# Masked attention: a cast moves from DVE to ScalarE, a subtraction moves behind the slot's second maximum, and four stages fetch their constants ahead of a norm

## The reference

```
x = x + tanh(g_xattn[l]) * attention_l(layernorm(x), context)
x = x + tanh(g_ffn[l])   * feed_forward_l(layernorm(x))
```

## Time and profile before

| | |
|---|---|
| Device time, median of 3 runs | 6104.12 us (6094.38 to 6107.08) |
| The profiled execution | 6067.9 us, span 6066.1 us |
| PE, DVE, ACT, POOL busy | 87%, 74%, 53%, 30% of the span |
| Granted TensorE clock, mean | 0.94 |
| Masked attention's loop | about 137 us to 1480 us of the span |

### The profile page before, as it was taken

How to read it: one execution, slowest core, us unless ns; L and a number is a source line. 1 busy time by engine, 2 the same in 40 slices (tenths; PEclk the granted TensorE clock), 3 DMA queues, 4 the chain that set the end, 5 groups by cost and what they waited for, 6 DMA issues and landing times. The chain is left out here.

```text
span 6066.1 us, 133138 instructions
## 1 busy us (share of the span) xinstructions
PE 5274.8 (87%) x51447; PEld 3802.1 (63%) x51447; DVE 4463.3 (74%) x9176; ACT 3196.1 (53%) x6024; POOL 1847.1 (30%) x1447
## 2 busy tenths in 40 slices
PE   3998998988679999989849999999999759999997
PEld 1777777777268878877824444444444437878885
DVE  7888888886367777763457777777777557777776
ACT  1666666666246666652224444444444226666663
POOL 5776767672122222212101111111111022222220
PEclk6999999999789999989969999999999879999998
DMA  5555555553267777742010000000000049889981
GB/s 128 131 125 128 125 129 127 126 128 76 49 129 139 135 142 142 140 88 105 25 31 20 16 15 15 15 15 15 15 15 10 8 101 158 158 163 162 162 157 25
DMA packets 369567, 545.00 MB, mean 90 GB/s; under 512 B 116084, under 2 KB 248310, under 8 KB 368806
## 3 DMA queue, kind: packets, MB, share of 16 engines
q1 hardware_dynamic: 366982, 533.81, 43.3%
q0 software_dynamic: 2048, 3.67, 0.2%
HBM read 413.45 MB, written 123.90 MB: 89 GB/s over the span
## 5 line engine op out<-in xcount | busy, mean ns | idle before, releaser
L696 DVE CUSTOM_DVE_ANT_0 attn_logits<-attn_scores,attn_shift 112x750 f32<-112x750 f32 x1024 | 945.6, 933 | 433.2 <-PE attn_scores L501 432.9
L614 ACT ACTIVATE attn_probs_t<-attn_pt 125x448 f32<-125x448 f32 x1536 | 831.0, 542 | 581.1 <-PE attn_pt L516 560.8
L516 PEld LDWEIGHTS attn_pt<-ident,attn_logits 112*125 112x125 f32 x6144 | 852.3, 189 | 178.6 <-issue 92.3
L516 PE MATMUL attn_pt<-ident,attn_logits 112*125 112x112 f32 x6144 | 921.1, 273 | 25.6 <-ACT attn_logits L605 24.5
L2329 PE MATMUL attn2k_pk<-attn_wk,attn2k_cn_t 128*125 128x512 f32 x1536 | 737.7, 602 | 39.6 <-ACT attn2k_cn_t L2400 36.8
L2340 PE MATMUL attn2k_pg<-attn2k_kn,attn2k_cn 125*128 125x512 f32 x1536 | 725.0, 594 | 4.5 <-ACT attn2k_gram L2408 2.3
L2495 DVE TENSOR_REDUCE attn2k_ss<-attn2k_sq 125x16 f32<-125x1024 f32 x384 | 467.0, 1216 | 255.2 <-ACT attn2k_sq L2437 255.1
L413 POOL CAST attn_k_parts<-xn_t 128x500 bf16<-128x500 f32 x192 | 206.5, 1075 | 1425.3 <-DVE xn_t L668 1425.3
L2437 ACT ACTIVATE attn2k_sq<-attn2k_pk 125x1024 f32<-125x1024 f32 x384 | 391.9, 1020 | 326.4 <-PE attn2k_pk L2329 326.2
L1228 ACT ACTIVATE attn_probs_t<-attn_pt 125x448 f32<-125x448 f32 x768 | 414.6, 540 | 281.2 <-PE attn_pt L1115 279.7
L2329 PEld LDWEIGHTS attn2k_pk<-attn_wk,attn2k_cn_t 128*125 128x125 f32 x1536 | 274.0, 187 | 399.2 <-issue 296.9
(11 more groups left out here) (371 smaller groups left out, 10444.4 us busy)
## 6 DMA issues: line engine op xcount, KB each, us to landing
attn_k_packed<-k_scratch SPq DMA_DIRECT2D x372, 375.0 KB, 6.3
attn_k_packed<-k_scratch SPq DMA_DIRECT2D x408, 187.5 KB, 4.4
k_scratch<-attn_k_parts SPq DMA_DIRECT2D x64, 1125.0 KB, 7.2
attn_ctx_t<-in_ctx_t SPq DMA_DIRECT2D x64, 750.0 KB, 7.3
k_scratch<-attn_k_parts SPq DMA_DIRECT2D x96, 375.0 KB, 3.7
attn_ctx_t<-in_ctx_t SPq DMA_DIRECT2D x96, 250.0 KB, 4.1
attn2k_ctx<-in_ctx SPq DMA_DIRECT2D x32, 750.0 KB
attn_mask_in<-in_mask SPq DMA_DIRECT2D x192, 109.4 KB
```

The source lines that it names most:

```text
L516: last = pe.transpose(pt[(3 * at + t) % 2][0:KC, (c % 4) * PAIR:(c % 4 + 1) * PAIR], logits[:, at % 3, c * KC:(c + 1) * KC], g.ident[0:PAI ...
L614: act.activation(probs_t[0:KC, p // 4, 4 * t:4 * t + 4, (p % 4) * PAIR:(p % 4 + 1) * PAIR], pt[(3 * at + t) % 2][0:KC, 0:QUAD].rearrange(" ...
L696: dve.tensor_tensor_reduce(out=logits[:, at % 3, cols].rearrange("p (b k) -> p b k", b=2), in0=scores[h][0:PAIR, :, 0:QTR], in1=shift[:, n ...
```

## The change

In the masked attention, `take_keys` on DVE keeps only the copy of the finite elements for the sequences from n = 2 on. The cast is issued by ACT (`high`), after the second `exp` and `lower` of slots 2 to 4 (and after `keep` in slot 2). The subtraction stays on DVE (`rest`), but stands behind the slot's second `shifted` instead of in front of it. For the first two sequences, which are prepared ahead of the loop, all three stay on DVE in the old order.

```
 ACT, slot p, after exp(.., 1) and lower(.., 1):
+    if t == 1 and 2 <= p < 5 and n + 2 < B:
+        high(n + 2, p - 2)
+def high(n, i):                      # on ACT
+    at = 3 * n + i
+    act.wait_ge(k_ready, at + 1)
+    if at > 1:
+        act.wait_ge(k_stored[at % 2], 16 * (at // 2))
+    act.activation(k_parts[:, at % 2, 0, :], clean_k[at % 2], ACT.Copy).then_inc(high_ready, 1)
 DVE, slot p:
     shifted(n, p, 0)
     take(n + 2, p - 2) ... finite ... mark
     shifted(n, p, 1)
+    if 2 <= p < 5 and n + 2 < B:
+        rest(n + 2, p - 2)
```

Four stages now take a function `ahead`, which is their norm. They allocate their SBUF tiles, issue their loads in Blocks of their own, in which nothing waits for the data, call `ahead()`, and allocate PSUM tiles and run as before:

```
+def fetch(nc, pairs, landed):
+    with nc.Block() as block:
+        @block.sync
+        def _(sp):
+            for dst, src in pairs:
+                sp.dma_start(dst, src).then_inc(landed, 16)
 ffn0:      fetch(6 loads); ahead()
 mixture:   fetch(router, order, bias); fetch(experts [, their bias]); ahead()
 attention2 (and ln1 gain and shift by a fetch before it, no longer waited for):
+  fetch(wv_t, wo, wq, wk, bo); fetch(gain, shift); fetch(first context tile); ahead()
 attn2q, first instructions of the engines:
+  DVE:  context_stats(0) in four steps, context_scales(0)
+  ACT:  context_root(0), context_normed(0) for all 12 chunks, then the copies of w_vo
+  POOL: context_affine(0), i.e. gain and shift
 attn2k: the same work for n = 0 is left out there; loads start with n = 1
```

More of the change, by code:

```diff
@@ L130, in _, with norm @@
                 act.wait_ge(tanhs, 1)
[L133 removed]
+def norm(nc, g, name, gate=None, out=None, twice=None, only_y=None, rows=None, twice_in=None):
     r = scope(nc, name)
@@ L1389, in take @@
                         take_keys(n, i)
+                        if n < 2:
+                            high(n, i)
+                            rest(n, i)
                     else:
@@ L1585, in ffn0 @@
                  (gate[:], a["gate0"].partition_broadcast(RANK))]
+        fetch(nc, loads, loaded)
+        ahead()
+        pw = [r.ps("pw0", [128, 512]), r.ps("pw1", [128, 512])]
+        pl = [r.ps("pl0", [128, 512]), r.ps("pl1", [128, 512])]
         def tensor(pe):
@@ L1679, in mixture @@
         values = lambda t: py[t % 3][0:PAIR, :, :].rearrange("p a (e d) -> p (a e) d", d=D)
-        with nc.Block() as block:
[L1681 to L1688, removed]
+        fetch(nc, [(wr[:], w_router), (order[:], a["c_order"].partition_broadcast(PAIR)),
+                   (br[:], b_router.partition_broadcast(PAIR))], loaded)
+        fetch(nc, [(we[:], w_experts.rearrange("e h d -> h e d"))] + ([] if b_experts is None else [(be[:], b_experts)]),
+              experts_in)
+        ahead()
+        pl, pb = r.ps("pl", [128, TILES, E]), r.ps("pb", [128, 512])
+        py = [r.ps(f"py{i}", [128, 2, 512]) for i in range(3)]
+        with nc.Block() as block:
             @block.tensor
@@ new lines, in attention2, with context_stats @@
+        ahead()
+        def context_stats(dve, n, j, half, step):
+            if step < 3:
+                if step == 0:
+                    dve.wait_ge(ctx_in[j], half * 16 + 16)
+                    wait(dve, steps, n * 3)
+                for c in range(4 * step, 4 * step + 4):
+                    last = dve.bn_stats(stats[:, c, :], ctx[:, j, c, :])
+                if step == 2:
+                    last.then_inc(steps, 1)
+                return
+            dve.wait_ge(steps, n * 3 + 1)
+            wait(dve, scale_ready, n)
+            dve.sem_inc(held, 1)
+            for c in range(CH):
+                last = dve.bn_aggr(mv[:, c, :], stats[:, c, :])
+            last.then_inc(steps, 1)
+            dve.wait_ge(steps, n * 3 + 2)
+            dve.tensor_scalar(var[:], mv[:, :, 1], EPS, None, ALU.add).then_inc(var_ready, 1)
@@ new lines, in context_scales, with context_root, context_normed @@
+        def context_scales(dve, n):
+            dve.wait_ge(root_ctx, n + 1)
+            wait(dve, raw_ready, n * CH)
+            dve.reciprocal(rs[:], var[:]).then_inc(steps, 1)
+            dve.wait_ge(steps, n * 3 + 3)
+            dve.scalar_tensor_tensor(off[:], mv[:, :, 0], -1.0, rs[:], ALU.mult, ALU.mult).then_inc(scale_ready, 1)
+        def context_root(act, n):
+            act.wait_ge(var_ready, n + 1)
+            act.activation(var[:], var[:], ACT.Sqrt).then_inc(root_ctx, 1)
+        def context_normed(act, n, j, chunks):
+            act.wait_ge(scale_ready, n + 1)
+            wait(act, summed, (n - 1) * CH)
+            for c in chunks:
+                act.activation(cn[:, j, c, :], ctx[:, j, c, :], ACT.Identity, bias=off[:, c:c + 1],
+                               scale=rs[:, c:c + 1]).then_inc(raw_ready, 1)
@@ L2238, in _ @@
                 def _(dve):
-                    chain = Chain(dve, steps)
+                    for step in range(4):
+                        context_stats(dve, 0, 0, 0, step)
+                    context_scales(dve, 0)
+                    chain = Chain(dve, q_steps)
                     def copy(t):
@@ L2632, in layout @@
     return out
-def loads(nc, name, pairs):
-    r = scope(nc, name)
-    with r.ctx:
-        loaded = r.sem("loaded")
-        with nc.Block() as block:
-            @block.sync
-            def _(sp):
-                for dst, src in pairs:
-                    sp.dma_start(dst[:], src).then_inc(loaded, 16)
-                sp.wait_ge(loaded, 16 * len(pairs))
 def program(nc, a, only=None):
@@ L2690, in program @@
                     part()
+            elif n % 2:
+                part(lambda: norm(nc, g, f"norm{n}", gate=gate))
             else:
```

195 lines of the change are left out of this document (83 added, 112 removed).

## The result

The changed kernel takes 6112.62 us (median of 20 runs, 6097.94 to 6126.78) against 6102.95 us (20 runs of the kernel before on the same chip): ratio 1.0016, 95% interval 1.0008 to 1.0023. It is slower by 10 us, less than the 12 us that this measurement was said to tell from no change, where 55 us of gain were predicted.

What follows compares the result with a forecast made beforehand. No engine was full: PE waited on DVE's maxima in the masked loop, and all engines on loads at the seams. Seams 33 us plus loop 22 us made 55 us off 6104, so 6049 us, range 5985 to 6084.

Steps and rivals of the forecast that it cites:

- The masked loop: Masked attention: an earlier second maximum gains 0.75 us a sequence (bounds 0.39 and 1.65), 22 us over 30 sequences.
- gained in any case: Masked loop, end of a sequence: PE's score had 0.39 us of slack over the last second maximum, the least gain.
- The three waits of PE: Masked loop, before the second scores of slots 3, 4 and 5: waits shrink from 3.94 to about 0.7 us a sequence.
- all of it moves to 938.85: Masked loop: POOL's unbroken work from its first split starts 1.3 us later and ends at 938.85 instead of 937.55.
- if POOL's chain gets shorter, because the DVE casts no longer stand in its way: Masked loop: the only source of more gain, up to 1.26 us, giving the upper bound of 1.65 us a sequence.
- from there on its chain is as before: Masked loop, slot 6: DVE waits for POOL's guard, then runs as before; the last second maximum ends at 946.27.
- The price of the cast: Masked loop, DVE: each of 90 casts priced at 0.46 us, not at the mean of some 0.72, its upper bound.
- The slower rival: Masked loop: POOL's chain binds, 3.2 us late from a late ACT, costing 45 us; 6116 us, chance 0.05.
- the loop gives nothing: Masked loop: POOL's chain starts another 0.4 us later and eats the 0.39; 6071 us, chance 0.19.
- The seams: Between stages: earlier loads save 33 us (25 to 38): 28.6 at layer 2's attention, 2.1 at ffn0, 2.4 at the mixtures.
- The base: Whole kernel: the profiled execution was 36 us faster than the median of 6104.12 us; the saving should be the same in both.
- The signs that were listed: Masked loop and seams: no DVE cast, shorter PE waits, later POOL split, about 42 us a sequence, both seam idle times gone.

Runs made afterwards that it cites:

- e5: Changed kernel with ScalarE's cast ahead of its second lowering of the slot and VectorE's subtraction ahead of the second maximum; ratio 1.0014 to the kernel before.
- e6: Changed kernel with GpSimd's low part of each key split cut to 8 of 500 columns, so it computes something else; ratio 0.9875 to the kernel before.
- e8: Changed kernel with the query-block product moved from GpSimd to ScalarE, as two copies in slot 6; ratio 0.9923 to the kernel before.
- e3: Changed kernel with GpSimd's query-block product placed behind guard 4 instead of ahead of it; ratio 1.0031 to the kernel before.
- e4: Changed kernel with the keys' cast back on VectorE, behind the slot's second maximum together with the subtraction; ratio 1.0013 to the kernel before.
- e2: Kernel before with the early loads alone, the masked loop as it was; ratio 0.9938 to the kernel before.
- e0: Kernel before, unchanged, profiled a second time; ratio 0.9998, trace span 6068.1 us.
- e11: Changed kernel, unedited, profiled again; ratio 1.0021 to the kernel before, trace span 6079.2 us.
- first pair: The first two traces compared, kernel before and changed kernel; the changed kernel's lasts 36 us longer.
- e7: Kernel before with the early loads alone, except that layer 2's attention issues its loads behind the norm; ratio 0.9968 to the kernel before.
- e9: Kernel before with the early loads and the query-block product on ScalarE instead of GpSimd; ratio 0.9972 to the kernel before.
- e1: Kernel before with the masked-attention part alone (ScalarE's cast, subtraction behind the second maximum); ratio 1.0066 to the kernel before.

## Why the prediction was wrong

**The masked loop is the step that failed.** The prediction took 0.75 us a sequence as a gain, with bounds 0.39 and 1.65, and it was 1.28 us lost. Even the 0.39 us, "gained in any case", did not come. Half of the mechanism had been named: POOL's split starts later by 1.3 us (measured 1.0), and DVE waits in slot 6 (2.09 us). The three waits of PE were to shrink from 3.94 to 0.7 us a sequence. The longest did shrink (3.1 to 2.0 us), but the sum of the earlier trace rows hardly did, 57.4 to 55.1 in 600 us. What was wrong were two statements about durations.

- "all of it moves to 938.85", and the bound above, "if POOL's chain gets shorter, because the DVE casts no longer stand in its way". The chain got 0.9 us longer: GpSimd's second and third cast went from 0.60 to 1.07 and 1.11 us and its product from 1.68 to 1.94, while the rest of the chain together took 0.3 us less. It does not come from the late start: in e5 the chain starts 0.8 us earlier than in the changed kernel and is longer still, 21.7 us. The chain was priced by its old durations, which held for the old neighbours only.
- "from there on its chain is as before". From the slot-6 copy to the next sequence it was 7.9 us and is 8.7: `finite` takes 0.81 instead of 0.41 us and the product with the reciprocal 0.87 instead of 0.39. Both now end just behind an instruction of guard 5, by 0.28 and 0.25 us. Before, `finite` ran beside guard 5's second clamp at its short length, and guard 5 had ended before the product.

Added up: 1.0 us later start, 0.9 us longer chain, less the 1.4 us by which VectorE used to come after guard 4, plus 0.8 us behind it: 1.3 us. The prediction counted 1.3 - 1.3 and stopped. The slack was right; the two terms beside it, 1.7 us together, were set to zero or below. The runs bear this out: taking 2.7 us (e6) or 1.8 us (e8) out of the chain gave 2.6 and 1.7 us of the period, while the runs that left all of GpSimd's work with it (e3, e4, e5) stayed at 44.2 to 44.4.

The Trainium skill has a rule that bears on this (SBUF — State Buffer, Who interferes with whom): when VectorE is in a mode that takes two ports, whichever of VectorE and GpSimd issues first holds the shared pair and the other one blocks fully, and a VectorE instruction with two inputs in SBUF contends with GpSimd's reads too. The traces agree in that instructions of both engines come out long: GpSimd's clamp took 2.67 us in e5 for 2.11 before, VectorE's two-input product 0.87 for 0.39. The prediction applied the rule to the cast that went and to `finite` behind it in slot 2. It did not apply it to GpSimd's own instructions, nor to VectorE's behind the copy of slot 6.

**The price of the cast** (0.46 us) was not what decided: e4 and the changed kernel show that the loop hardly feels it (44.33 and 44.11 us) while GpSimd's chain binds.

**The slower rival** ("POOL's chain binds") had 0.05 and was the right mechanism, for another reason than the one given, a late ScalarE: e4, without ScalarE's cast, is as slow. The rival "the loop gives nothing" stopped at zero. The case that came true, a longer chain and a longer tail behind it, had no number, though the earlier trace rows held one: the same cast took 0.42 us in the median and 1.49 at most.

**The seams were right in sum.** 33 us were predicted; e2's runs give 38 us (30 to 46), the pair e0 and e11 gives 31 and the first pair 35. The same terms of e2's trace come to 31 us against e0, but that trace lost 15 us in ffn0 (see the end), so as a whole it is only 20 us shorter.

| term | predicted | e0 to e11 | first pair |
|---|---|---|---|
| ffn0, last score to attn1's first keys | -2.1 | -1.5 | -3.8 |
| ahead of the `w_vo` products (-10.7 + 5.3) | -5.4 | -6.0 | -6.6 |
| products to queries | +3.2 | +3.0 | +3.0 |
| queries' end to the first transpose | -28.6 | -29.2 | -28.9 |
| context loop, with the wait for the second tile | +2.2 | +4.2 | +2.4 |
| two mixtures | -2.4 | -1.4 | -1.4 |

The wait for the second tile is 2.42 us, as said (2.30 in e11, where the loop took 1.8 us more for reasons not looked into). The earlier mixture gave nothing: the norm ahead of it starts 3 us later, which the prediction had left out there, and the stage behind it begins 3 us sooner.

**The base.** The 36 us between the first profile and the median were rightly left out of the sum, but no cause was asked for. The traces put 32 us of such a difference into ffn1.

**The signs that were listed** mostly came: no VectorE cast, ScalarE's of 0.62 us, the split later, the wait in slot 6, both idle times at the seams gone. Two did not: the window of a sequence is 44.0 us, not 42, and PE's waits of 0.52, 0.39 and 3.03 us were not gone or under 1 us but came back ahead of the second scores of slots 5, 6 and 7, with 1.3, 1.6 and 1.1 us on average.

## What to carry to other kernels

The durations of VectorE's and GpSimd's instructions in these traces depend on what runs beside them (`finite` takes 0.41 to 1.88 us). So before you price a move on one of the two, list what will newly run beside the other's chain and price those instructions at their long form. If an engine's chain binds, moving its work to a later place may change little (e3), while taking work off the engine paid nearly one for one (e6, e8). Compare traces stage by stage, and ask of any stage whose code is the same why it differs: here 32 us had nothing to do with the change.

## What the runs showed that I had not expected

- ffn1's first part takes 75 to 76 us in nine traces and 105 to 108 us in five, always with the level of before's runs on that chip, whatever the change.
- In e2, e7 and e9 it is 15 us longer than in the kernel before from ffn0's first product to attn1's first keys, in e1 and e3 10 us. The granted clock shows it, with the same 96 matmuls in the window (e2, then before; PE's busy time first, the clock third from the end):

```profile
1553.00:1616.00 63.00, 62.17 (x96) 20.89 (x96) 2.12 (x4) 18.14 (x33) 0.00 (x0) 0.68 0.00 0
```
```profile
1560.00:1609.00 49.00, 47.48 (x96) 16.56 (x96) 2.50 (x4) 17.93 (x32) 0.00 (x0) 0.90 0.00 0
```

  The cause is open, and it may be a matter of single executions: the profiled ones of e2, e7 and e9 are 12 to 15 us slower than the medians of their runs (6050.4 against 6037.9 us in e2), so the ratios need not contain it.
